# Queries, keys and values of a windowed attention loaded by 17 DMAs per chunk in place of 3, without the masked copies

## The reference

```
h = tok(x); h = concatenate([h, txt], axis=1)          # 64 x 273 x 256
Q, K, V = proj(layernorm(h))                           # (n, head, s, d), 16 heads of 16
attn = softmax(einsum('nqhd,nkhd->nhqk', Q, K) / 4)    # q and k run over the 16 heads of one token
out = einsum('nhql,nlhd->nqhd', attn, V); h = h + out @ Wo.T + bo
h = h + ffn(layernorm(h))                              # sigmoid gate, squared relu, mix with the token before
```

## Time and profile before

| what | value |
|---|---|
| time of the profiled execution | 1723.9 us |
| its span | 1722.2 us |
| the three runs | 1718.64 to 1731.56 us, median 1730.68 us |
| TensorE busy | 1481.2 us, 86% |
| VectorE busy | 1323.2 us, 77% |
| ScalarE busy | 1260.7 us, 73% |
| GpSimd busy | 933.9 us, 54% |
| DMA packets | 698,051, of them 612,862 under 512 bytes |

### The profile page before, as it was taken

One profiled execution on the slowest core, in us unless ns is written; L12 is line 12 of the kernel. 1 busy time (PEld: TensorE's weight loads), 2 busy tenths in 40 slices (PEclk: granted clock), 3 DMA queues, 4 the chain that ended last, 5 costly groups with the idle time before them and its releaser, 6 DMA issues.

```text
span 1722.2 us, 53654 instructions
## 1 busy us (share of the span) xinstructions
PE 1481.2 (86%) x18772; PEld 1404.6 (82%) x18772; DVE 1323.2 (77%) x3097; ACT 1260.7 (73%) x2401; POOL 933.9 (54%) x1508
## 2 busy tenths in 40 slices
PE   4686898989989899989989899998988988898866
PEld 4586798888888888888889888888988888888855
DVE  5666788787888787878878778887887878787642
ACT  2255787787788788777778877887877777786753
POOL 3121356556656555655655665565565556556547
PEclk8788899999999999999999999999999999999988
DMA  4267767877887876886697779788678877878651
GB/s 117 56 119 130 122 140 142 131 143 135 154 139 143 148 144 129 147 140 127 142 149 142 131 148 149 141 149 128 142 140 139 141 136 144 135 151 133 122 84 35
DMA packets 698051, 227.64 MB, mean 132 GB/s; under 512 B 612862, under 2 KB 669246, under 8 KB 697786
## 3 DMA queue, kind: packets, MB, share of 16 engines
q1 hardware_dynamic: 697786, 224.22, 72.5%
HBM read 121.64 MB, written 89.64 MB: 123 GB/s over the span
## 4 chain that ended last, share of the span: by engine, by line
PE 26%; SPq 21%; DMA 18%; ACT 10%; issue 10%; DVE 5%; POOL 1%; ACTq 0%; POOLq 0%; DVEq 0%
PE bank L976 13%; SPq L495 10%; DMA vd<-qkv_dram 7%; DMA on<-o_dram 5%; SPq L451 4%; PE bank L1050 3%; SPq L505 3%; ACT arena L873 3%; PE bank L1070 3%; DMA qk<-qkv_dram 3%; PE bank L1029 2%; ACT pt L883 2%; PE bank L1102 1%; DVE probs L732 1%; DMA o_dram<-probs 1%
## 5 line engine op out<-in xcount | busy, mean ns | idle before, releaser
L976 PE MATMUL bank<-wqkv,xnT 128*126 128x384 f32 (+1 forms) x1728 | 346.5, 345 | 3.7 <-issue 3.0
L1070 PE MATMUL bank<-wtok,xT 128*98 128x258 f32 x2304 | 311.7, 291 | 17.8 <-DVE xT L744 14.9
L1070 PEld LDWEIGHTS bank<-wtok,xT 128*98 128x98 f32 x2304 | 291.4, 171 | 22.7 <-DVE xT L744 19.7
L976 PEld LDWEIGHTS bank<-wqkv,xnT 128*126 128x126 f32 (+1 forms) x1728 | 293.4, 185 | 12.1 <-issue 6.2
L628 POOL TENSOR_TENSOR mixp<-mixf,mixp 128x364 fp32r<-128x364 f32 x192 | 186.3, 981 | 161.9 <-ACT mixp L950 159.9
L867 ACT ACTIVATE arena<-qk,ymask 128x768 f32<-128x768 f32 x192 | 165.5, 930 | 57.4 <-DMA qk<-qkv_dram 57.4
L873 ACT ACTIVATE arena<-vd,ymask 128x768 f32<-128x768 f32 x192 | 173.8, 958 | 23.4 <-DMA vd<-qkv_dram 23.4
L893 ACT ACTIVATE xcols<-xim 84x640 f32<-84x640 f32 (+1 forms) x192 | 131.8, 694 | 47.4 <-DMA xim<-in_x 47.1
L815 DVE TENSOR_TENSOR qkvt<-bank,bqkv 126x384 f32<-126x384 f32 (+1 forms) x288 | 154.0, 544 | 13.7 <-PE bank L976 12.1
L844 DVE SCALAR_TENSOR_TENSOR mixf<-dT,mus,zT 128x364 f32<-128x364 f32 x192 | 123.9, 666 | 36.2 <-POOL zT L622 31.3
L572 POOL TENSOR_TENSOR rs<-ve,small 126x3 f32<-126x3 f32 (+1 forms) x160 | 140.3, 877 | 12.5
(11 more groups left out here) (118 smaller groups left out, 3603.0 us busy)
## 6 DMA issues: line engine op xcount, KB each, us to landing
xim<-in_x SPq DMA_DIRECT2D x128, 294.0 KB
qk<-qkv_dram SPq DMA_DIRECT2D x48, 768.0 KB, 7.9
qkv_dram<-qkvt SPq DMA_DIRECT2D x96, 378.0 KB
vd<-qkv_dram SPq DMA_DIRECT2D x96, 192.0 KB, 7.2
qkv_dram<-qkvt SPq DMA_DIRECT2D x48, 336.0 KB
o_dram<-probs SPq DMA_DIRECT2D x288, 48.0 KB, 1.8
out<-h SPq DMA_DIRECT2D x96, 126.0 KB
on<-o_dram SPq DMA_DIRECT2D x64, 126.0 KB
```

The source lines that it names most:

```text
L976: ins = mm(psum, left(a, k), right(b, k), start=t == 0, stop=t == len(terms) - 1)
L1070: ins = mm(place("tok", c)[0:PT, 0:E + 2], xT[:, a, i0:i0 + GRID // 2, :].rearrange("p i w -> p (i w)"), wtok[:, b, ch, :], start=t == 0, ...
```

## The change

Keys and values are no longer copied by ScalarE. `kb` and `vb` are cleared once, and each of eight DMAs writes the keys of one token position of eight (16 partitions) into that token's block of `kb`; the same for the values and `vb`. Queries come by one DMA of their own into `qd`. The order table and the banks are new, with `k_in` as a new step. The clearing of `pt2` goes from GpSimd to VectorE, and VectorE clears the 6336 columns of `arena` when the weights are done.

```diff
-        qk = sb("qk", [128, GR, 2 * HD])
-        vd = sb("vd", [128, GR, HD])
+        qd = sb("qd", [128, GR, HD])
...
                     for k in due(q, s, "qk_in", 0):
                         after_all(qkv_out, q, k)
-                        after(kb_sb, q, k - 1, 4)
                         after(q_sb, q, k - 1, 2)
-                        src = qkv_dram[k % CPQ, :, :, 0:2 * HD]
-                        qk_in.done(sp.dma_start(qk[:, :, :], src.rearrange("(g t) i j -> (t i) g j", t=8)))
+                        src = qkv_dram[k % CPQ, :, :, 0:HD]
+                        q_in.done(sp.dma_start(qd[:, :, :], src.rearrange("(g t) i j -> (t i) g j", t=8)))
+                    for k in due(q, s, "k_in", 0):
+                        if q * CPQ + k == 0:
+                            sp.wait_ge(prep_dve, DVE_ALL)
+                        after_all(qkv_out, q, k)
+                        after(s_pe, q, k - 1, PARTS)
+                        src = qkv_dram[k % CPQ, :, :, HD:2 * HD].rearrange("(g t) i j -> t i g j", t=8)
+                        for t in range(8):
+                            k_in.done(sp.dma_start(kb[HD * t:HD * t + HD, :, t % 4, :], src[t]))
                     for k in due(q, s, "v_in", 0):
+                        if q * CPQ + k == 0:
+                            sp.wait_ge(prep_dve, DVE_ALL)
                         after_all(qkv_out, q, k)
-                        after(vb_sb, q, k - 1, 4)
-                        src = qkv_dram[k % CPQ, :, :, 2 * HD:QKV].rearrange("(r g y) i j -> r (y i) g j", r=2, y=4)
+                        after(av_pe, q, k - 1, PARTS)
+                        src = qkv_dram[k % CPQ, :, :, 2 * HD:QKV].rearrange("(r g y) i j -> r y i g j", r=2, y=4)
                         for rr in range(2):
-                            v_in.done(sp.dma_start(vd[64 * rr:64 * rr + 64, :, :], src[rr]))
+                            for yy in range(4):
+                                p = 64 * rr + HEADS * yy
+                                v_in.done(sp.dma_start(vb[p:p + HEADS, :, yy, 0:HD], src[rr, yy]))
...
-            for t in (hc, mv3, mv4, qx, pt2, zT):
+            for t in (hc, mv3, mv4, qx, zT):
...
+            c = prep(V.memset(pt2[:], 0.0))
...
+                c = prep(V.memset(arena[:, :], 0.0))
...
-                    for yy in range(4):
-                        for k in due(q, s, "kspread", yy):
-                            if yy == 0:
-                                qk_in.wait(act, q, k, 1)
-                                s_pe.wait(act, q, k - 1, PARTS)
-                            kb_sb.done(A.activation(kb[:, :, yy, :], qk[:, :, HD:2 * HD], ACT.Copy, scale=ymask[:, yy:yy + 1]))
-                    for yy in range(4):
-                        for k in due(q, s, "vspread", yy):
-                            if yy == 0:
-                                v_in.wait(act, q, k, 2)
-                                av_pe.wait(act, q, k - 1, PARTS)
-                            vb_sb.done(A.activation(vb[:, :, yy, 0:HD], vd[:, :, :], ACT.Copy, scale=ymask[:, yy:yy + 1]))
...
-                                kb_sb.wait(pe, q, k, 4)
+                                k_in.wait(pe, q, k, 8)
...
-                                vb_sb.wait(pe, q, k, 4)
+                                v_in.wait(pe, q, k, 8)
```

More of the change, by code:

```diff
@@ L50 @@
 SLOT, IMG, QUAD = 4000, 3000, 12000
[L51 to L65, removed]
@@ L67 @@
-BANK = dict(x=[3, 6, 5], tok=[5, 6], stat=[3], xt=[7, 0], qkv=[1, 2, 7, 2, 0, 7], s=[0, 4], pt=[1, 4], av=[7, 4],
-    ont=[0, 1], wo=[1, 7, 4], zt=[4, 0], k=[2, 4], r=[2, 1, 7], val=[0, 2, 4])
+AT = dict(load=[0], xcols=[1070, 1089, 1363], sq=[2092], ssq=[2421], sqm=[3198, 3344], x=[1152, 1293, 1551],
+    xh=[1425, 1990, 1993], xl=[1701, 2002, 2041], tok=[2219, 2957], stat=[2691], statc=[3259], statr=[3309],
+    rstd1=[3583], txt=[8126], yn=[3685, 3744], st2=[3825, 4054], mv2=[4289, 4408], rstd2=[5256], hg=[4541, 5494],
+    h=[5970, 6082], hdma=[7219], st3=[10367, 10446, 10476], mv3=[10513, 10632, 10690], rstd3=[11352], xn=[11476,
+    11739, 11818], xt=[11946, 11949], xnh=[11995, 12080], xnl=[12109, 12256], hb=[16279], qkv=[12470, 12766, 13084,
+    13637, 13921, 14142], qb=[12659, 13356, 13636, 13935, 14231, 14394], qkv_out=[13696, 14448, 14681],
+    qk_in=[15598], v_in=[16958], qplace=[16304, 16571], s=[16933, 16938], mx=[17044, 17072], sub=[17198, 17297],
+    exp=[17202, 17399], pt=[17470, 17572], ptc=[17495, 17604, 17711, 17831], av=[17659, 17871], rec=[17969, 18008],
+    osb=[18038, 18039], o_out=[18630], o_in=[23137], ont=[23760, 23857], onh=[23853, 23939], onl=[23929, 23982],
+    wo=[24059, 24155, 24369], h2=[24269, 24300, 24455], st4=[24674, 24911, 25607], mv4=[25429, 25867, 25870],
+    rstd4=[26171], z=[26174, 26215, 26271], zt=[26331, 26399], carry=[26073], ztc=[26903, 26954], d=[27053, 27068],
+    edge=[27075], mix=[27379, 27384, 27862, 28116], mixh=[27439, 27679, 28513, 28795], mixl=[27826, 27913, 29028,
+    29419], k=[28017, 28479], kr=[28705, 28911], ksq=[29414, 30059], kah=[30001, 30168], kal=[30229, 30235],
+    r=[30676, 30754, 30987], rt=[31261, 31378, 31393], val=[31163, 31331, 31730], rv=[31424, 31555, 31733],
+    add=[32003, 32790, 33460], out=[33099, 33258, 34394], k_in=[15604])
@@ L69 @@
+BANK = dict(x=[6, 1, 7], tok=[6, 1], stat=[7], xt=[4, 5], qkv=[5, 4, 2, 3, 2, 3], s=[3, 0], pt=[0, 5], av=[0, 4],
+    ont=[0, 2], wo=[2, 0, 7], zt=[4, 2], k=[3, 2], r=[5, 3, 0], val=[4, 5, 3])
 PE_ORDER = ("s", "pt", "av", "x", "tok", "stat", "xt", "qkv", "ont", "wo", "zt", "k", "r", "val")
@@ L475, in body @@
                             if i == 0:
-                                after(qk_in, q, k - CPQ, 1)
-                                after(v_in, q, k - CPQ, 2)
+                                after(q_in, q, k - CPQ, 1)
+                                after(k_in, q, k - CPQ, 8)
+                                after(v_in, q, k - CPQ, 8)
                             qkv_out.done(k, sp.dma_start(qkv_dram[k % CPQ, o:o + rows, :, :].rearrange("t i j -> t (i j)"), qkvt[0:rows, i, :]))
@@ L515, in _ @@
             out_dma.wait(sp, QUADS - 1, CPQ - 1, 3)
-            qk_in.wait(sp, QUADS - 1, CPQ - 1, 1)
-            v_in.wait(sp, QUADS - 1, CPQ - 1, 2)
+            q_in.wait(sp, QUADS - 1, CPQ - 1, 1)
+            k_in.wait(sp, QUADS - 1, CPQ - 1, 8)
+            v_in.wait(sp, QUADS - 1, CPQ - 1, 8)
             on_in.wait(sp, QUADS - 1, CPQ - 1, ROW_DMAS)
@@ L798, in body @@
                         for k in due(q, s, "qplace", xx):
-                            qk_in.wait(dve, q, k, 1)
+                            q_in.wait(dve, q, k, 1)
                             s_pe.wait(dve, q, k - 1, PARTS)
@@ L802, in body @@
                             half = slice(64 * xx, 64 * xx + 64)
-                            q_sb.done(V.tensor_copy(qx[half, :, xx, :], qk[half, :, 0:HD]))
+                            q_sb.done(V.tensor_copy(qx[half, :, xx, :], qd[half, :, :]))
                     for kk in range(2):
```

16 lines of the change are left out of this document (8 added, 8 removed).

## The result

The changed kernel takes **1900.53 us** (median of 4 runs, 1888.23 to 1907.05), the kernel before 1727.16 (4 runs, 1718.64 to 1731.56): ratio 1.100, 95% interval 1.093 to 1.108. Forecast were 1687 us and faster, in a range that ended at 1790. The profiled execution took 1907.05 us, 183 more than that of before.

The account below looks back on a forecast made before the run. No engine was taken as full: a closed chunk loop of 32.7 us through several engines bound the kernel, with SP next. 48 x (31.8 - 32.7) = -43, plus 6.5 once, turned 1723.9 into 1687 us; range 1635 to 1790.

Parts of the forecast that it names:

- the price of the loads: On SP's queue: three loads at 3.8 us each, 11.4 in place of 8.7, so 2.7 us a chunk more.
- the value burst: Profiled value load: 64-byte pieces at 115 GB/s, 1.8 a ns, giving 3.4 us for 6144 pieces.
- the long burst: Profiled 128-byte pieces at 154 GB/s, 1.2 a ns, giving 5.1 us for 6144 or 0.64 a DMA.
- the first rival: On SP's queue: small DMAs are slow, SP held 0.64 us by each of 16, 1855 us; chance 27%.
- The 8.7 of before: SP's hold by the old loads a chunk: 4.3 us for queries and keys, 4.4 for the value pair.
- The loop through the scaling: Chunk loop through output DMAs, loads, TensorE and VectorE: some 5 us of slack, SP's 2.8 us scaling wait goes.
- my 26.6 us: Length forecast for the new chunk loop, from output DMAs through loads and landing to TensorE and VectorE.
- 30.2 + 1.6 = 31.8: Forecast chunk time on SP: 30.2 us of its own work plus 1.6 of waits for others.
- the estimate from it, 19.0: Loads on SP if overhead equals transfer time: keys and values 7.6 us each, 19.0 in place of 11.4.
- The second rival: At scores or value product: waits only change place, a chunk keeps 32.7 to 32.8 us, up to 1735; chance 20%.
- The third: TensorE is the bound, SP no obstacle: a chunk takes 30.5 us, 1625 us in all; chance 12%.
- The new order, priced at nothing: Order table: serves TensorE's largest wait, 1.8 us a chunk, but counted as no gain beyond the loop.

Follow-up runs that it names:

- e2: Kernel before, with queries and keys loaded by two DMAs of 6144 64-byte pieces each instead of one of 128-byte pieces, copies kept: 1898.23 us (1.100).
- e7: Kernel before, with only the queries loaded, 6144 pieces of 64 bytes instead of 128, keys left out, all instructions kept: 1728.5 us (1.003).
- e11: Kernel before, its loads and masked copies kept, in the changed kernel's order and banks, value load at 16023: 1802.6 us (1.042).

## Why the prediction was wrong

**The step that failed: the price of the loads**, "I take 3.8 a load, 0.47 a DMA ... That is 11.4 in place of 8.7". Measured are 16.8, 5.4 us a chunk more than I took. Four things were mis-sized.

- *A load of 6144 pieces of 64 bytes.* Two of them in e2 hold the DMA behind them for 3.8 and 5.7 us in the chunk shown (its chain in order of time) where one 128-byte load had held it for 4.3. I took the piece rate from the value burst, 1.8 a ns, because it had the same piece size; by e7 the size is no argument, and the slower rate of the long burst, 1.2, was the nearer row. The additional load was entered at 3.8 and the two old ones cheapened by 0.5 and 0.6; e7, with such a cheaper load, gained nothing.
- *A DMA of 768 pieces.* Undisturbed they stand 0.56 us apart, not the 0.45 of the output DMAs that I used: those have fewer pieces each, at most 250 (what the loads' 590 thousand leave of 698 thousand packets, over 432 DMAs). The 0.51 above which I said that the first rival decides was passed by the plain issue, before any stall.
- *Stalls.* The first key DMA waits 3.5 us for the query load, later ones take 1.1 to 3.2. I paid the hold between loads once, in the price of a load, and eight DMAs have eight places to meet it.
- *The 8.7 of before.* The value pair of 2.53 that I called undisturbed is the shortest of 38 from 400 to 1600 us; their mean is 5.95. With the means of these rows in the same sum the old loads cost some 10 us a chunk (an estimate). That is why SP's issues rose by 7.1 and not by 16.8 - 8.7 = 8.1.

**"The loop through the scaling has some 5 us of slack"** was wrong; that this loop would still be closed I had named as what would make me wrong. SP's wait for the scaling, which was to fall under 1 us a chunk, is 55.5 us in 1300, 1.6 a chunk. Against my 26.6 us the loop in the chain has 37.8: output DMAs 5.7 for 3.5, the stretch to the query load 3.3 for 4.6, loads 18.5 for 11.4, the image load between 1.2 for 2.2, landing 4.8 for 1.8, TensorE 3.2 for 2.0, VectorE 1.2 for 1.1. Of 11.2 too little, 7.1 are the loads and 3.0 the landing, where I used the 1.8 of the output DMAs for a DMA whose pieces stand behind seven others'.

**What held.** The form of the sum did: SP's work plus the waits that are left. Forecast 30.2 + 1.6 = 31.8, measured 32.2 of issues and 2.8 of gaps plus 1.9 of waits, 36.9: the work is 4.8 too small, 5.4 for the loads less 0.6 elsewhere. That the waits came near the forecast is luck: I had dropped the wait for the scaling and kept 1.6 of the others, and what is left is 1.6 for the scaling and 0.3 for the products. From the first output DMA to the last a chunk took 1714.6 / 47 = 36.5 us; 4.7 more than forecast, over 47 chunks, are 220 us, the distance from 1687 to 1907. ScalarE lost 327 of the 339 us. The start cost 8.9 where I had 6.5.

**The first rival** (small DMAs are slow, 27%) came nearest, with both marks that I gave it: 5 us or more for a group of eight, and SP as the bound. But its name covers only a part, as e2 has no small DMA and loses as much as the change. Its price, 15.7, was below the 16.8 measured, and its 1855 us too low; the range, which left out its slow half, ended at 1790. The Trainium skill (DMA: Bandwidth & Descriptors, Rules for kernel authors) advises to join transfers under 64 KB, and I set the estimate from it, 19.0 for the loads where 16.8 were measured, aside for a row of unlike DMAs. The direction was the page's. e2 shows that its reason, overhead of small transfers, is the smaller part here: splitting one full transfer into two of 384 KB costs more than going on from four DMAs to seventeen with the pieces unchanged (173 against 106, half of that the remainder of the table).

**The second rival** had a true part: TensorE waits for `arena<-qkv_dram` at L1052, 46.3 us from 400 to 1700, 1.3 a chunk, over my mark of 1. But SP's own waits fell instead of staying whole, and a chunk took 36.5 us and not 33. **The third**, TensorE as the bound, is refuted by its 82%.

**The new order, priced at nothing.** It is not nothing: -25 to +76 us depending on the loads beside it, with the reserves named at e11. An order is fitted to the durations around it; I valued one wait that it serves and not those that it opens.

## What to carry to other kernels

Count pieces before bytes: where a load was cut into runs of 128 bytes, halving the run while keeping the bytes about doubled its price here, and removing engine work that was mostly hidden doesn't pay for that. Price a new DMA by a row with the same number of pieces, not the same size in KB; and if the queue that issues it is on the path, enter its hold on the next DMA at every place where one follows another. An order of steps is worth testing with the durations that it was made for, since the same order gave -25 us in one kernel and +76 in another.
